# Edge counting in a graph layer: spans of 12 nodes and groups of four chunks in place of 16 and three

## The reference

```python
xn = _layernorm(x, axis=-1)
x = x + gnn(xn, edge_index, W, b) + mix(xn[None], Wq, bq, Wk, bk, Wv, bv, Wo, bo)[0]
x = x + ffn(_layernorm(x, axis=-1)[None], clip_x, clip_down, w_gate, w_up, w_down)[0]

# gnn: self loops, symmetric norm, relu
deg = segment_sum(ones_like(dst), dst, num_segments=n)
norm = rsqrt(deg)[src] * rsqrt(deg)[dst]
out = relu(segment_sum((xn @ W)[src] * norm[:, None], dst, num_segments=n) + b)

# mix: q, k with relu, 16 heads of 64
context = einsum('bhld,bhkd->bhlk', q, k) / (l * DH)
attn = einsum('bhlk,bhkd->bhld', context, v)
```

## Time and profile before

| | |
|---|---|
| time, median of 3 runs (range) | 785.83 us (784.84 to 786.09) |
| the profiled execution, its time | 784.87 us |
| its span | 783.0 us |
| TensorE busy, matmuls | 738.4 us, 94% of the span |
| VectorE busy | 535.9 us, 68% |
| GpSimd busy | 257.1 us, 33% |
| ScalarE busy | 235.5 us, 30% |
| TensorE's granted clock, mean | 0.979 |

### The profile page before, as it was taken

One profiled execution on the slowest core, in us unless ns is written; L12 is line 12 of the kernel. 1 busy time (PEld: TensorE's weight loads), 2 busy tenths in 40 slices (PEclk: granted clock), 3 DMA queues, 4 the chain that ended last, 5 costly groups with the idle time before them and its releaser, 6 DMA issues.

```text
span 783.0 us, 12879 instructions
## 1 busy us (share of the span) xinstructions
PE 738.4 (94%) x3904; PEld 378.6 (48%) x3904; DVE 535.9 (68%) x1052; ACT 235.5 (30%) x419; POOL 257.1 (33%) x397
## 2 busy tenths in 40 slices
PE   5999999989999999999999999999999999966965
PEld 2455555545555554666544444444444444433532
DVE  7878888888777766667821111677777788746687
ACT  5133335553333345556111111401101110005520
POOL 5456466766666655550100000111111111100016
PEclk9999999999999999999999999999999999996987
DMA  9401001441000000003020300501111110000005
GB/s 343 184 28 56 28 21 55 161 162 55 0 0 0 0 2 0 2 0 109 13 95 0 108 0 0 162 21 58 56 50 48 48 56 28 21 0 1 1 27 235
DMA packets 17985, 43.67 MB, mean 56 GB/s; under 512 B 1702, under 2 KB 2734, under 8 KB 17940
## 3 DMA queue, kind: packets, MB, share of 16 engines
q1 hardware_dynamic: 17940, 43.08, 16.1%
HBM read 37.96 MB, written 5.12 MB: 55 GB/s over the span
## 4 chain that ended last, share of the span: by engine, by line
PE 77%; DVE 9%; issue 7%; ACT 2%; DVEq 2%; POOL 1%; DMA 1%; POOLq 0%; SPq 0%; ACTq 0%
PE bank L487 30%; PE bank L563 13%; PE bank L694 12%; PE bank L668 10%; PE bank L730 4%; PE bank L472 2%; DVE counts L1062 2%; PE bank L627 2%; PE bank L504 1%; DVE mem L973 1%; DVEq L1054 1%; ACT mem L781 1%; DVE mem L1353 1%; DMA mem<-in_x 1%; PE bank L745 1%
## 5 line engine op out<-in xcount | busy, mean ns | idle before, releaser
L487 PE MATMUL bank<-mem 128*128 128x512 f16 x1440 | 330.2, 381 | 1.8 <-ACT mem L781 1.7
L487 PEld LDWEIGHTS bank<-mem 128*128 (+1 forms) x1440 | 138.5, 98 | 150.8 <-issue 5.1
L396 POOL TENSOR_SCALAR hot_src<-iota_p,src_col 125x128 bf16<-125x128 bf16 x220 | 151.2, 698 | 18.4 <-issue 18.4
L1062 DVE TENSOR_TENSOR counts<-bank,counts 128x160 f32 x324 | 104.9, 324 | 62.4 <-issue 29.1
L563 PE MATMUL bank<-mem 128*128 128x384 f16 (+1 forms) x576 | 108.8, 343 | 0.0
L694 PE MATMUL bank<-mem 128*128 128x512 f16 x480 | 105.2, 379 | 0.0
L668 PE MATMUL bank<-mem 128*128 128x512 f16 x400 | 88.0, 379 | 0.0
L800 ACT ACTIVATE src_gap<-iota_p,loT 125x128 bf16<-125x128 bf16 x110 | 44.0, 400 | 136.0 <-PE bank L472 123.8
L563 PEld LDWEIGHTS bank<-mem 128*128 128x128 f16 (+1 forms) x576 | 55.4, 98 | 42.0
L694 PEld LDWEIGHTS bank<-mem 128*128 128x128 f16 x480 | 46.7, 98 | 54.6
L1049 DVE TENSOR_TENSOR hot_dst<-iota_w,keyT 125x480 bf16<-125x480 bf16 x110 | 71.5, 651 | 0.1
(11 more groups left out here) (148 smaller groups left out, 696.1 us busy)
## 6 DMA issues: line engine op xcount, KB each, us to landing
mem<-in_x SPq DMA_DIRECT2D x18, 512.0 KB, 3.3
out_x<-mem SPq DMA_DIRECT2D x9, 512.0 KB
mem<-in_L_mix_Wk SPq DMA_DIRECT2D x4, 1024.0 KB, 9.4
mem<-in_L_mix_Wv SPq DMA_DIRECT2D x4, 1024.0 KB, 8.1
mem<-in_L_mix_Wq SPq DMA_DIRECT2D x4, 1024.0 KB, 5.3
mem<-in_L_gnn_W SPq DMA_DIRECT2D x4, 1024.0 KB, 5.1
mem<-in_L_mix_Wo SPq DMA_DIRECT2D x2, 2048.0 KB, 8.4
mem<-in_L_ffn_w_down SPq DMA_DIRECT2D x4, 352.0 KB, 3.0
```

Of the source, the lines that this page charges most:

```text
L396: pool.tensor_scalar(hot_src[0:EC, i, c, :], iota_p[0:EC, :], src_col[0:EC, i, c:c + 1], None, ALU.is_equal).then_inc(S["hot_src_ready"], 1)
L487: last = pe.matmul(o[:, :], xT[:, a * K + k, bass.ds(t * P, P)], w16[i][:, k, b, :], start=(at == 0), stop=(at == len(parts) - 1))
L1062: dve.tensor_tensor(window, agg[i][:, k * WC:(k + 1) * WC], window, ALU.add).then_inc(S["adj_added"], 1)
```

## The change

The windows get 12 nodes (120 columns) in place of 16 (160), and the groups four chunks in place of three, so a bank and the `hot_dst` buffer hold 480 columns as before. The groups are spread anew: a tile of K and V has three in place of four, late ones four in place of five, the query blocks 12 and 8 in place of 16 and 12. That is 82 groups and 328 chunks in place of 108 and 324. A K unit now has one group in the tiles with three, behind its 12th matmul, and V has two, behind the 10th and the 22nd; (0,2) has three in V, behind the 4th, 14th and 24th. A late tile has two and two. Since `G - 1` is now 3, GpSimd makes three `hot_src` matrices of a group and ScalarE still one.

```diff
-W = 16
+W = 12
 WC = W * T
 WINDOWS = -(-N // W)
-G = 3
-KV_GROUPS, LATE_GROUPS, Q_GROUPS = 4, 5, (16, 12)
+G = 4
+KV_GROUPS, LATE_GROUPS, Q_GROUPS = 3, 4, (12, 8)
 GROUPS = T * KV_GROUPS + (T - 2) * LATE_GROUPS + sum(Q_GROUPS)
 CP = GROUPS * G
...
-        GROUP_AT = {0: (), 2: (10, 22), 3: (4, 14, 24), 4: (6, 12, 18, 24)}
+        GROUP_AT = {0: (), 1: (12,), 2: (10, 22), 3: (4, 14, 24), 4: (6, 12, 18, 24)}
```

## The result

The changed kernel takes **775.59 us**, median of 4 runs (774.95 to 776.98), against 785.34 (783.87 to 786.09) for the kernel before; the ratio is 0.9876, 95% interval 0.986 to 0.9891. That is 9.75 us faster. The profiled execution was its slowest run, 776.98 us with a span of 775.2.

What follows compares the result with a forecast made beforehand. TensorE, busy 94% of the span, was taken as the bound, with VectorE late in the weight-conversion tiles. From 784.87 us, 5.3 of columns and 4.2 of stalls gave 775.4, stated as 776.0; range 772.0 to 781.5.

Steps and rivals of the forecast that it cites:

- Matmul columns: TensorE's count groups: a chunk falls from 0.070 to 0.053 us, saving 5.3 us, bounds 4.7 to 8.8.
- The load sets the pace: Rival for the count matmuls: weight load keeps a chunk at 0.070 us, only stalls pay, 781.0 us; chance 0.05.
- the sustained figure: Skill's 81 ns for a weight load and 128-column matmul; would make count chunks 26.6 us, 3.9 more than now.
- Stalls: TensorE's waits on one-hot rows in weight tiles and first counted tile: 4.2 of 5.48 us go, bounds 0 and 5.5.
- The walk: VectorE followed through tiles from 124.70 us: rows late only around 169 and 176 us, 1.25 of 4.45 us stays.
- the sentence on distances: Rows follow the adds of the group two before; that distance grows from 24 matmuls to at least 26, removing stalls.
- the K evacuation no longer stands behind a K group: Second reason given for fewer stalls in the weight tiles: K's evacuation on VectorE no longer follows a K group.
- Only the columns pay: Rival: stalls stay, as a chain over ScalarE's high parts and VectorE's low parts; 779.6 us, chance 0.20.
- GpSimd: One-hots in late tiles: a group takes 2.30 us against a spacing of 3.03, so covered with 0.7 us to spare.
- Layernorm's rstd: GpSimd's third one-hot delays it by 0.6 us and VectorE waits; slack of 2.4 us a tile, so no cost.
- The sum: Whole kernel: 784.87 - 5.3 - 4.2 = 775.4 us; median expected at 775.4 to 776.3, stated as 776.0.

Runs made afterwards that it cites:

- the rows of 80 and 40 columns: Two kernels: the changed kernel with count matmuls and adds cut to 80 or 40 of 120 columns, results wrong; 769.34 and 766.54 us.
- crowded groups: The changed kernel with one group of a unit behind matmul 23 instead of 12, two behind 2 and 12 instead of 10 and 22; 779.43 us.
- less work in the old places: The kernel before with spans of 12 nodes alone, keeping groups of three chunks, 108 groups and their places; 776.73 us.
- the repeated run: The changed kernel unaltered, run once more beside other kernels on one chip; 775.03 us.

## Why the prediction was right, by its steps

- *Matmul columns, 5.3 us.* Right: 5.3 in the stretch, 0.0525 us a chunk for 0.053. It stands on the 96-column transposes; nothing else in the trace showed that the 128 columns of weight load hide behind so short a stream.
- *The load sets the pace* (0.05): wrong, shown by 0.0525 us a chunk and by the rows of 80 and 40 columns. With it falls, for this stream, the sustained figure that the prediction set beside it from the Trainium skill, "TensorE: Matmul & The Clock Gate", section "Back-to-back issue gap".
- *Stalls, 4.2 of 5.5 us.* 4.39. The walk put 1.25 us of lateness at about 169 and 176 us (0.75 and 0.5); it was 1.09, at 169.54 and 176.59 (0.55 and 0.54). The single add was forecast at 0.281 us (0.324 - 0.043) and took 0.282.
- *Why they go.* That the places of the groups count beside the work is shown: crowded groups with equal work bring 4.7 us back, and less work in the old places leaves 3.2. The add's width alone is worth 1.5. Two reasons in this part are not borne out as given. The distance to the group two before is not the measure: 4.9 of the crowded kernel's stalls are at groups where it is 24 matmuls or more, as it is in the changed kernel. What the traces show is when VectorE gets to the adds of that group, behind a low part (and ScalarE's high part before it) or an evacuation. The walk through VectorE's list had this in it, and so found the two late places; the sentence on distances did not. And "the K evacuation no longer stands behind a K group" is no reason: with two groups in K again, and other distances with them, the stalls all but vanish.
- *Only the columns pay* (0.20, 779.6): out by the stretch, in which 4.39 us of stalls went, and by the same two kernels.
- *GpSimd.* That it is covered was right, but the margin was looked for in the wrong place. I priced it by the late tiles and a one-hot of 0.61 us; there it has more room than I gave (61 one-hots in 35.07 us from 196.7 to 257.2, 0.575 each by busy time). The tight place is the weight tiles, where a one-hot stretches to over 2 us. The mean over the kernel lay above the calm one and said so.
- *Layernorm's rstd, costed at nothing.* Between 40 and 370 us VectorE now waits for it 5.4 us in six tiles, where it waited once, for 0.7; the plain tile is still 12.77 us, so it costs nothing.
- *The sum.* 784.87 - 9.7 is 775.2 by the stretch. The profiled execution was 776.98, since its start was 1.8 us late; the others, 774.95 to 775.59, lie where the sum put them.

## What to carry to other kernels

Read the price of a narrow matmul from its nearest relatives in the same trace, here transposes, with their next instruction's start, before trusting a figure from elsewhere. Where an engine feeds TensorE through two buffers, a stall is set by where the units of work stand as much as by the work: find the tightest place, also across a tile's border and where the pattern changes. Counting the matmuls between them is not enough: write down in order what the feeding engine does in between, since one long instruction in front of the adds (2.29 us here) made a group 1.67 us late at a distance that elsewhere cost nothing. Look for an engine's margin where its instructions are stretched by a neighbour, not where it is calm.

## What the runs showed of the hardware

In the first profile after, TensorE had the full clock from 20 to 32 us, but from 32.00 to 39.30 us a granted clock of 0.77, a mean of stretches at 2.4 and at 1.2 GHz; the part at half clock is the second line:

```profile
32.00:39.30 7.30, 7.30 (x30) 3.25 (x29) 4.31 (x9) 1.60 (x3) 0.55 (x1) 0.77 0.24 75
32.40:35.80 3.40, 3.40 (x10) 1.20 (x9) 2.73 (x5) 1.29 (x3) 0.00 (x0) 0.50 0.51 159
```

Less than a microsecond before it fell, TensorE had stood idle for 1.90 us:

```profile
31.51 1.17 PE L460 MATMUL bank<-ident,mem 128*128 128x128 f32 x8 [1.90 <-DVE mem L957]
32.47 6.99 PE L487 MATMUL bank<-mem 128*128 128x512 f16 x24
```

The 24 projection matmuls took 6.99 us there; before, after an idle time of 1.08 us, they took 5.34, and 5.34 in the repeated run, after 0.56. The idle time belongs to a part that the change doesn't touch, and its length varies between executions. Whether the idle time is what lowered the clock was not tried, and the other runs leave it open. The kernel with two more one-hots on GpSimd fell to half clock after an idle time of 2.26 us. The one with one more stood idle for 2.28 us before 175.92 and kept the full clock. The second run of two groups in K fell at 378.8 us with no idle time listed from 371 us on, behind 20 matmuls of one column, and the first run of the same kernel, with the same work there, did not. Such a stretch at half clock costs 1.6 to 1.7 us here (6.99 against 5.34 us, 775.62 against 773.91).
